# Taking the square roots of q and k ahead of later evacuations in ScalarE's order

## The reference, cut to what matters

```python
def l2norm(t):
    return t / jnp.clip(jnp.linalg.norm(t, axis=-1, keepdims=True), 1e-12)
...
def _layer(x, wqkv, qs, ksc, wo, lg, lb, w1, b1, w2, b2):
    h = shift_token(x)
    qkv = h @ wqkv
    q, k, v = jnp.split(qkv, 3, axis=-1)
    ...
    q = l2norm(q) * qs
    k = l2norm(k) * ksc
    q, k = rotary_xpos(q, k)
    o = local_attention(q, k, v)
    ...
    x = x + o @ wo
    ...
    return x
```

## Time and profile before

| | |
|---|---|
| median of 16 runs | 3032.3 us (3025.47 to 3251.95) |
| the profiled execution | 3030.74 us |
| its slowest core, from first to last instruction | 3029.2 us |
| spans of the 8 cores | 3005.6 to 3029.2 us |
| TensorE busy with matmuls | 2061.1 us, 68% |
| VectorE busy | 1094.4 us, 36% |
| ScalarE busy | 602.4 us, 20% |
| GpSimd busy | 34.6 us, 1% |

### The profile page before, as it was taken

How to read it: one execution, slowest core, us unless ns; L and a number is a source line. 1 busy time by engine, 2 the same in 40 slices (tenths; PEclk the granted TensorE clock), 3 DMA queues, 4 the chain that set the end, 5 groups by cost and what they waited for, 6 DMA issues and landing times.

```text
span 3029.2 us, 27642 instructions; the slowest of 8 cores (3005.6 to 3029.2 us)
## 1 busy us (share of the span) xinstructions
PE 2061.1 (68%) x9366; PEld 934.7 (31%) x9488; DVE 1094.4 (36%) x1849; ACT 602.4 (20%) x1016; POOL 34.6 (1%) x50
## 2 busy tenths in 40 slices
PE   1166576699756675999224667758997577759993
PEld 1122233244322331444111223323442223323442
DVE  4804445411125446111374144453111244452112
ACT  1032231210023331110022233312100233312100
POOL 0000000000010000000000000000000000000000
PEclk9996556799885557999557855568998755569996
DMA  4248920122369700212332300001212200001223
GB/s 83 73 52 100 111 34 28 35 76 56 44 71 111 83 1 28 71 60 79 111 104 36 42 0 1 1 28 44 76 57 40 35 1 1 1 28 63 67 64 113
DMA packets 123855, 159.73 MB, mean 53 GB/s; under 512 B 48211, under 2 KB 90708, under 8 KB 122500
## 3 DMA queue, kind: packets, MB, share of 16 engines
q0 software_dynamic: 30624, 52.42, 14.9%
q1 hardware_dynamic: 93092, 105.53, 12.0%
HBM read 201.95 MB, written 44.03 MB: 81 GB/s over the span
## 4 chain that ended last, share of the span: by engine, by line
PE 59%; DVE 23%; ACT 6%; issue 5%; DMA 4%; SPq 2%; DVEq 1%; ACTq 0%
PE psA L1619 10%; DVE UN L333 8%; PE psA L1177 8%; PE psA L1602 5%; PE psA L1598 5%; PE psB L1602 5%; PE psB L1598 4%; DVE Bb L333 4%; PE psB L956 4%; DVE attnT L333 4%; PE psA L867 4%; PE psB L1216 3%; PE psB L867 2%; PE psA L1329 2%; DMA out<-UN 2%
## 5 line engine op out<-in xcount | busy, mean ns | idle before, releaser
L333 ACT ACT_TABLE_LOAD x67 | 86.0, 1283 | 1172.5 <-PE psA L1177 368.8
L1602 PE MATMUL psB<-stg,WS 128*128 128x512 bf16 x704 | 277.7, 395 | 24.6 <-ACT stg L333 23.2
L1598 PE MATMUL psB<-stg,WS 128*128 128x512 bf16 x672 | 264.4, 394 | 28.2 <-ACT stg L333 28.2
L1602 PE MATMUL psA<-stg,WS 128*128 128x512 bf16 (+1 forms) x704 | 269.1, 382 | 1.3
L1598 PE MATMUL psA<-stg,WS 128*128 128x512 bf16 (+1 forms) x680 | 260.5, 383 | 0.0
L1619 PE MATMUL psA<-Bb,WS 128*128 128x512 bf16 x1000 | 230.1, 386 | 13.7 <-DVE UN L333 12.7
L1177 PE MATMUL psA<-Bb 64*128 64x128 bf16 (+3 forms) x432 | 179.3, 415 | 34.9 <-ACT probs L333 30.0
L333 ACT ACTIVATE probs<-psA 128x640 bf16<-128x640 f32 (+5 forms) x264 | 171.4, 649 | 95.1 <-PE psA L1177 68.2
L1216 PE MATMUL psB<-attnT,Bb 128*64 128x128 bf16 x960 | 79.1, 311 | 144.1 <-DVE attnT L333 144.1
L333 DVE TENSOR_TENSOR UN<-UN 128x1024 bf16<-128x1024 bf16 (+1 forms) x48 | 41.7, 870 | 313.3 <-ACT UN L333 275.7
L867 PE MATMUL psA<-stg,WS 128*128 128x512 bf16 x502 | 129.5, 416 | 36.2 <-DVE stg L333 20.7
(11 more groups left out here) (118 smaller groups left out, 2470.1 us busy)
## 6 DMA issues: line engine op xcount, KB each, us to landing
WS<-wpre SPq DMA_DIRECT2D x184, 256.0 KB, 2.9
wpre<-w1p POOLq DMA_DIRECT2D x8, 2730.0 KB, 71.1
WS<-wpre SPq DMA_DIRECT2D x96, 224.0 KB
UN<-x SPq DMA_DIRECT2D x32, 512.0 KB, 4.7
WS<-wqkv POOLq DMA_DIRECT2D x24, 512.0 KB, 5.8
wpre<-w2p POOLq DMA_DIRECT2D x4, 2730.0 KB, 145.8
out<-UN SPq DMA_DIRECT2D x16, 512.0 KB, 5.6
Bb<-c_tabhi SPq DMA_DIRECT2D x8, 512.0 KB
```

Of the source, the lines that this page charges most:

```text
L333: ins = f(*a, **kw)
L1598: t.matmul(rA[0:ln, tc * 512:(tc + 1) * 512], wu[:, kt * ln:(kt + 1) * ln], B.stg[kt][:, tc * 512:(tc + 1) * 512], start=(kt == 0), stop=( ...
L1602: ins = t.matmul(rG[0:ln, tc * 512:(tc + 1) * 512], wu[:, 1024 + kt * ln:1024 + (kt + 1) * ln], B.stg[kt][:, tc * 512:(tc + 1) * 512], sta ...
```

## The change

On ScalarE, Ln and Exp of q are moved from behind the evacuations of chunks 8 to 11 to behind that of chunk 3, and Ln and Exp of k to behind that of chunk 7. The counts computed ahead are renumbered to fit the new order. The other engines' programs are not touched; the counts that they wait for change with the tables. The whole diff:

```diff
--- before.py
+++ after.py
@@ -787,18 +787,15 @@
 
         sb = B.sS.n
         B.qs8_ev = (B.sS, sb + 1)
-        qevac_pred = [(B.sS, sb + 2 + c) for c in range(8)]
-        vevac_pred = [(B.sS, sb + 10 + c) for c in range(4)]
-        sqrt_pred = [(B.sS, sb + 15), (B.sS, sb + 17)]
-        rot_pred = [None] * 8
-        vev_pred = [None] * 4
-        pos = sb + 17
-        for g_ in range(4):
-            rot_pred[g_] = (B.sS, pos + 1)
-            vev_pred[g_] = (B.sS, pos + 9)
-            pos += 9
-        for g_ in range(4):
-            rot_pred[4 + g_] = (B.sS, pos + 1 + g_)
+        qevac_pred = [None] * 8
+        for c in range(4):
+            qevac_pred[c] = (B.sS, sb + 2 + c)
+            qevac_pred[4 + c] = (B.sS, sb + 8 + c)
+        sqrt_pred = [(B.sS, sb + 7), (B.sS, sb + 13)]
+        vevac_pred = [(B.sS, sb + 14 + c) for c in range(4)]
+        rot_pred = [(B.sS, sb + 18 + 9 * g_) for g_ in range(4)] + \
+            [(B.sS, sb + 54 + i) for i in range(4)]
+        vev_pred = [(B.sS, sb + 26 + 9 * g_) for g_ in range(4)]
         B.vev_ev = vev_pred
         B.vevac_pred = vevac_pred
         B.rot_pred = rot_pred
@@ -1031,17 +1028,12 @@
             B.w(sc, "scalar", B.lcols_ev)
             ev = B.ev(B.sS, sc.mul(B.qs8[:], B.qs8[:], 8.0))
             assert ev == B.qs8_ev, (ev, B.qs8_ev)
-            for c in range(8):
-                B.w(sc, "scalar", mm_ev[c])
-                ev = B.ev(B.sS, sc.activation(
-                    rawb(c), reg_of(c % 3), AF.Identity))
-                assert ev == qevac_pred[c], (ev, qevac_pred[c])
-            for c in range(8, 12):
-                B.w(sc, "scalar", mm_ev[c])
-                ev = B.ev(B.sS, sc.activation(vdm(c - 8), reg_of(c % 3),
-                                              AF.Identity))
-                assert ev == vevac_pred[c - 8], (ev, vevac_pred[c - 8])
             for qk in range(2):
+                for c in range(4 * qk, 4 * qk + 4):
+                    B.w(sc, "scalar", mm_ev[c])
+                    ev = B.ev(B.sS, sc.activation(
+                        rawb(c), reg_of(c % 3), AF.Identity))
+                    assert ev == qevac_pred[c], (ev, qevac_pred[c])
                 B.w(sc, "scalar", n2done[qk])
                 dst = B.rq[:] if qk == 0 else B.rk40[32:40, :]
                 p0 = 0 if qk == 0 else 32
@@ -1049,6 +1041,11 @@
                 B.ev(B.sS, sc.activation(dst, n2, AF.Ln, bias=1e-30))
                 ev = B.ev(B.sS, sc.activation(dst, dst, AF.Exp, scale=0.5))
                 assert ev == sqrt_pred[qk], (ev, sqrt_pred[qk])
+            for c in range(8, 12):
+                B.w(sc, "scalar", mm_ev[c])
+                ev = B.ev(B.sS, sc.activation(vdm(c - 8), reg_of(c % 3),
+                                              AF.Identity))
+                assert ev == vevac_pred[c - 8], (ev, vevac_pred[c - 8])
             for c in range(8):
                 B.w(sc, "scalar", rotmm_ev[c])
                 pb = (c % 2) * 1024
```

## The result

The changed kernel takes 2946.94 us (median of 9 runs) against 3031.72 (48 runs): ratio 0.9719, with a 95% interval of 0.9696 to 0.9742. The forecast was 2949. Some executions of this and other kernels ran with a lower granted clock on the cores of one die; the medians count them, the ratios leave them out, and where no ratio is given the time is that of the profiled execution (for the changed kernel 2946.34 us, for the kernel before 3030.74).

A forecast was written before the change was run, and what follows sets the result against it. The prediction took TensorE's waits to set the time, 73.8 us of them before the first products. 3030.74 - 72.9 (gap) - 8.4 (clock) = 2949 us, range 2922 to 2975.

The forecast's parts named there:

- The gap is one serial chain: TensorE's 18.45 us idle before each query-key-value stage's first product, ending on VectorE's clamps and reciprocals; 72.9 us saved together.
- TensorE and VectorE end together: Before the first product, VectorE's reciprocals end 0.4 us after chunk 11 in stage one; TensorE is last in stages two, four.
- The pairs cost nothing: ScalarE's early Ln and Exp, 2.25 us a pair, stay hidden: 2.4 us to spare before chunk 4, 1.3 before chunk 8.
- No table load: On ScalarE, the order Identity, Ln, Exp, Identity adds no function-table load; by rows, loads would cost under 1 us per stage.
- The clock: First product and first rotation of each stage run at full clock once the gap closes: 2.1 us a stage, 8.4 us.
- still just inside: First rotation ends at most 4.7 us behind chunk 11, within 4.8 us of full clock; 0.4 us more a stage.
- The rival in which the full clock lasts through all products: TensorE never falls to half clock through products and rotations: 52 us more saved, 2897 us; chance 8%.
- Nothing given back: Copied feed-forward weights have 102 us of slack against 20, other work moves forward, so no saved time is lost later.

The follow-up runs named there:

- The halves alone: Against the kernel before, only q's Ln and Exp moved early: 3005.56 us, ratio 0.9921; only k's moved early: 3028.26 us.
- the gap put back: Changed kernel with eight more value-preserving clamps on VectorE behind k's reciprocal in each stage: 2980.43 us, ratio 0.9862.

## Why the prediction was right, point by point

- **The gap is one serial chain, and it goes but for 0.8 us**: right. 72.9 us were forecast for the four stages; the idle time fell by 73.0. The halves alone (25 and 2 us) and the order of before without reciprocals (gaps of 6.55) show that it is VectorE's run that was hidden and that q's root starts it.
- **TensorE and VectorE end together**: right in size, wrong in place. I had the first and third stage 0.4 us late; on the core profiled it was the first and fourth. Where the clock's dip falls decides: chunk 8 took 4.84 us in the second and third stage, which moves chunk 11 behind VectorE's run, and 3.63 in the first and fourth; before the change (another core) it was the second and fourth that had the slow chunk 8.
- **The pairs cost nothing**: right for this kernel, with less room than I wrote. I read 2.4 us of room behind q's pair from one stage in which chunk 4 started at half clock; at full clock it is 1.4 us, and beyond it each microsecond costs TensorE more than one, since the clock falls as well. Behind k's pair a delay of 5.4 us is taken up by the three PSUM regions.
- **No table load**: right, 67 loads in both. The Trainium skill (ScalarE: Activation LUTs, Rules for kernel authors) asks to group activations by table set and counts about 2.7 us for every switch to a different set. The prediction took that to speak against this order; the trace shows no switch between Identity, Ln and Exp, so the rule had nothing to say here.
- **The clock**: right for the first product, in part luck in size, 9.2 us for 8.4. From the first product to the second it is now 4.79, 4.69, 4.71 and 5.39 us; before it was 7.20, 7.18, 7.20 and 7.19. Of the 9.2 us the products gave 7.1 (1.8 a stage, for 1.7 forecast). The rotation, forecast at full clock in every stage, was so in three, and the transposes behind it, for which nothing was forecast, gained there too; in the fourth stage the clock reads 0.50 from 2333.1 us on, 2.4 us behind chunk 11, and the rotation gained nothing. The 4.8 us by which the rotation was to be "still just inside" was read from one gap and did not hold there; what sets it no run shows. With the gap put back the 9.2 us came back. The rival in which the full clock lasts through all products is out: 0.50 from the second product on, with TensorE busy 35.67 of 47.90 us. The Trainium skill (TensorE: Matmul & The Clock Gate, Part 1) says that activity releases the slow clock; these float32 matmuls, with the small bf16 ones between them, did not, nor did the float32 ones alone in the earlier trace rows.
- **Nothing given back**: right. 73.0 + 9.2 = 82.2 us are accounted for, of 84.4 between the two profiled executions; the 2.2 left are within what executions of one kernel differ by (2.0 of them a shorter wait for weights ahead of the stages' first chunks, 12.4 us in place of 14.4).

## What to carry to other kernels

When a wait ends on a slow engine's serial run, look for what starts that run: here 4.5 us of ScalarE work in the wrong place held back 14.8 us of VectorE work, and moving one half alone gave almost nothing (k) or less than a third (q). Before a wait is put in the middle of an in-order queue, measure the room at the consumer behind it, at the faster of its clocks; the same delay cost 27 us ahead of chunk 4 and about 4 ahead of chunk 8. And once the gap is closed, the next wait is one that was not on the list of the first: here the eight small waits for the sums, worth as much again.

## What was not expected of the hardware

The price of an idle stretch of TensorE went beyond the stretch: a gap of 5 to 7 us cost about 2.3 us more up to the second product, and a wait of 7.5 us about 1.6 us more in the chunks, both through the granted clock. When the clock falls was not the same from stage to stage: 2.4 us behind chunk 11 in the fourth stage of the changed kernel, with the first product between, and 4.9 us behind it in the first. The float32 product of 8 rows took 1.95 us at full clock against 3.75, so it does scale with the clock, but a stage that is three quarters busy with such products and small matmuls stayed at 0.50.
